# A decoder layer with a second cross attention: a new order of the same work on four engines

## The chip, the cores and the metric

The kernel runs on one core of one Trainium2 chip, in one launch. A core has a matrix engine (TensorE, PE in the profile, its weight loads PEld), three engines for elementwise work (VectorE or DVE, ScalarE or ACT, GpSimd or POOL) and a queue that issues the transfers (SyncE, SP). Each takes its instructions strictly in the order in which they are written, and waits on semaphores for the others. The metric is the device time of one execution in microseconds: median of three runs 888.63, lowest 887.2, highest 890.95.

## The reference

What is computed, for 64 sequences of 64 tokens with 256 features and 16 heads of 16:

```
def _L0(x, enc, self_mask, cross_mask, ...):
    q, k, v = split(layernorm(x, ln1) @ w_qkv + b_qkv)
    x = x + merge(attention(q, k, v, self_mask)) @ w_ao + b_ao
    q = layernorm(x, ln2) @ w_q + b_q
    k, v = split(enc @ w_kv + b_kv)
    x = x + merge(attention(q, k, v, cross_mask)) @ w_co + b_co
    return x + gelu(layernorm(x, ln3) @ w1 + b1) @ w2 + b2        # w1: 256 x 1024
def _L1(x, enc, mask, ...):
    a = norm(enc) * ln_gamma + ln_beta
    out = softmax(where(mask, (x @ Wq.T) (a @ Wk.T)^T * scale, -inf)) (a @ Wv.T)
    return x + tanh(gate) * (out @ Wo.T)
x = _L1(_L0(x, ctx, mask1, mask2, ...), ctx, mask3, ...)
```

Scores are `scores * mask - 10000 * (1 - mask)` in the first two attentions; everything is float32.

## The kernel before, in words

The 64 sequences are 16 units of 4 (256 tokens). A unit passes four working stages in four successive rounds: A is the self attention, B the first cross attention, M the MLP with the keys' and values' side of the second one, C the second cross attention. P, ahead of A, is the norm of the loaded tokens. In a full round (`steady`, 13 of them, the last without P) all stages work, each on another unit. Rounds 0 to 3 (`fill0` to `fill3`) fill the pipeline, `drain1` to `drain3` empty it. During `fill1` and `fill2` the weights are split into a high part (ScalarE, `high_weights`) and a low part (VectorE, `low_weights`).

Each matrix product of a projection is made of three: high times high, high times low, low times high. So an operand is turned on TensorE (`turn`), its high part is written by ScalarE (`high_part`), its low part by VectorE (`low_part`), and a projection (`feature_major` for queries, keys and the MLP's four inner parts H0 to H3; `token_major` for values and outputs) is twelve matmuls, of which the last four wait for the low part.

An attention x goes through these steps. TensorE: `scores(x, t)`, two halves of two pieces each. VectorE: `mask_scores(x, r)` for piece r = 0 to 3, `row_max`. GpSimd: `add_offset` (A and B), `shift` (subtract the row maximum). TensorE: `turn_probs(x, r)`, the transposed piece. ScalarE: `exps`, the exponential. TensorE: `values(x, t)`. VectorE: `normalise`. TensorE: `turn_out` (x.OT), then ScalarE's and VectorE's high and low part of it, then the output projection x.AO. VectorE's `tokens_out` adds the residual that GpSimd prepared (`residual`), `moments` takes mean and variance, GpSimd's `rstds` the inverse root, ScalarE's `normalised` applies both. The MLP: `gelus` on ScalarE, `high_h` on VectorE, `low_h` on GpSimd, then `mlp_out(t, part)` on TensorE.

What the order hangs on: every engine's list for each kind of round is written out by hand in `fill1` ... `drain3`. Two tables go with them. `PJ_ORDER` says in which order projections and turns claim the four projection banks of PSUM; a use waits until the use four places earlier has been read out (`claim`). `S_ORDER` says the same for the four score banks, which the scores and the turned pieces of A, B and C share. The keys `k2` and queries `q2` are one buffer each for all three attentions, so A's keys wait for B's scores. A and C share the buffer of probabilities. `keep_busy` is four transposes whose result nobody reads. `carry_shifts` makes bias columns out of the norms' shifts and the weights; `finish_biases` adds them up on VectorE.

## Time and profile before

| what | value |
|---|---|
| median of three runs | 888.63 us (887.2 to 890.95) |
| the profiled execution | 887.42 us, its span 885.6 us, mean granted TensorE clock 0.99 |
| TensorE matmuls, weight loads | busy 850.9 us (96%), 813.2 us (92%) |
| VectorE, ScalarE, GpSimd | busy 660.4 (75%), 573.8 (65%), 557.4 us (63%) |
| DMA | 26.76 MB, mean 30 GB/s |
| longest waits in total | GpSimd for the variance 200.3 us, ScalarE for the turned output 88.3, GpSimd for C's row maxima 82.7 |
| table loads on ScalarE | 63 of 1.28 us |

The span runs from the first to the last instruction; the execution's own time is 1.8 us more. Busy times of different engines overlap, so they are not parts of a sum. An engine's idle time costs nothing unless the engine that sets the end waits for it. The first filling round ends near 43.6 us, the second near 84, the third at 130.1; the full rounds run to 792.9, the first emptying round to 834.8, the second to 862.6.

### The profile page before, as it was taken

The numbers are of one execution on the slowest core, as the hardware profiler recorded it, in microseconds if no ns is written. First come the engines' busy times: TensorE is split into PE (matmuls) and PEld (weight loads), VectorE is DVE, ScalarE is ACT, GpSimd is POOL, SyncE is SP. The second block draws the span as 40 slices with busy tenths as digits, with TensorE's granted clock in tenths as the row PEclk, the third lists the DMA queues.
The fourth block names the chain that finished last, engine by engine and source line by source line (L and its number), as shares of the span: only waits on it lengthen the run. The fifth ranks groups of instructions, "written<-read, shape, count | busy, mean of one in ns | idle before, by whom it ended". The sixth has DMA issues, their size and how long they took to land.

```text
span 885.6 us, 24680 instructions
## 1 busy us (share of the span) xinstructions
PE 850.9 (96%) x9940; PEld 813.2 (92%) x9940; DVE 660.4 (75%) x1474; ACT 573.8 (65%) x1083; POOL 557.4 (63%) x565
## 2 busy tenths in 40 slices
PE   7878999999999999999999999999999999999996
PEld 7877889999999999999999999999999999998885
DVE  5868758778787777877777778778787787778454
ACT  5544858577584848758484866758485775848443
POOL 1456756749294765929486683938567492956351
PEclk9889999999999999999999999999999999999999
DMA  9010100100101010110101010010101001010000
GB/s 298 7 31 15 45 1 14 46 13 9 49 3 45 14 45 13 32 28 2 44 14 45 13 46 14 2 46 13 45 13 46 14 7 39 2 45 2 27 13 13
DMA packets 34143, 26.76 MB, mean 30 GB/s; under 512 B 12784, under 2 KB 33392, under 8 KB 34032
## 3 DMA queue, kind: packets, MB, share of 16 engines
q1 hardware_dynamic: 34032, 25.20, 9.8%
q8 instruction: 80, 1.31, 0.6%
q14 instruction: 31, 0.25, 0.1%
HBM read 20.99 MB, written 4.19 MB: 28 GB/s over the span
## 4 chain that ended last, share of the span: by engine, by line
POOL 44%; PE 34%; DVE 10%; issue 6%; ACT 4%; DMA 0%; POOLq 0%; SPq 0%; DVEq 0%; ACTq 0%
POOL prob_AC L1897 11%; POOL prob_B L1891 8%; POOL h_lo L1904 8%; POOL prob_AC L1891 8%; POOL prob_B L1897 5%; PE s_bank L566 5%; PE s_bank L541 4%; PE pj L439 3%; PE pj L492 3%; POOL rstd L1877 3%; PE pj L500 2%; PE pj L494 2%; PE pj L470 2%; PE pj L478 2%; PE pj L472 2%
## 5 line engine op out<-in xcount | busy, mean ns | idle before, releaser
L1877 POOL TENSOR_TENSOR rstd<-var_eps,half 128x2 f32<-128x2 f32 x64 | 45.5, 711 | 200.3 <-DVE var_eps L1402 200.3
L1897 POOL TENSOR_TENSOR prob_AC<-prob_AC,rmax_C 128x512 f32<-128x512 f32 x64 | 68.5, 1072 | 82.8 <-DVE rmax_C L1356 82.7
L1008 ACT ACTIVATE prob_AC<-s_bank 128x512 f32<-128x512 f32 x128 | 73.7, 616 | 70.7 <-PE s_bank L552 70.5
L1000 ACT ACTIVATE k<-pj,kbias,consts 128x256 f32<-128x256 f32 x192 | 92.7, 566 | 31.2 <-PE pj L478 26.6
L541 PE MATMUL s_bank<-k,q 64*128 64x128 f32 x1536 | 102.0, 282 | 6.3 <-ACT q L987 4.4
L541 PEld LDWEIGHTS s_bank<-k,q 64*128 64x128 f32 x1536 | 91.9, 190 | 13.6 <-ACT q L987 4.8
L1891 POOL TENSOR_TENSOR prob_AC<-prob_AC,maskA_off 128x512 f32<-128x512 f32 x64 | 81.5, 1286 | 15.0 <-DVE prob_AC L1351 15.0
L1891 POOL TENSOR_TENSOR prob_B<-prob_B,maskB_off 128x512 f32<-128x512 f32 x64 | 82.2, 1295 | 6.8 <-DVE prob_B L1351 6.5
L960 ACT ACTIVATE oT_AC_hi<-pj,bias 128x256 fp32r<-128x256 f32 x64 | 26.9, 472 | 88.3 <-PE pj L579 88.3
L1904 POOL TENSOR_TENSOR h_lo<-g,h_hi 128x512 fp32r<-128x512 f32 x64 | 82.4, 1296 | 1.2 <-DVE h_hi L1862 1.2
L552 PE MATMUL s_bank<-consts,prob_AC 128*128 128x128 f32 x512 | 72.9, 275 | 9.0 <-POOL prob_AC L1897 7.8
L552 PEld LDWEIGHTS s_bank<-consts,prob_AC 128*128 128x128 f32 x512 | 56.7, 140 | 16.5 <-issue 13.8
L1365 DVE RECIPROCAL rden<-s_bank 128x16 f32<-128x16 f32 x96 | 24.5, 256 | 61.6 <-PE s_bank L566 61.2
L1897 POOL TENSOR_TENSOR prob_B<-prob_B,rmax_B 128x512 f32<-128x512 f32 x64 | 69.0, 1088 | 0.8 <-DVE rmax_B L1356 0.8
L566 PEld LDWEIGHTS s_bank<-vz_AC,prob_AC 128*64 128x64 f32 x2048 | 62.6, 138 | 6.8 <-issue 4.0
L566 PE MATMUL s_bank<-vz_AC,prob_AC 128*64 128x34 f32 x2048 | 66.5, 225 | 1.4 <-issue 0.7
L513 PE MATMUL pj<-w_hi_M,h_hi 128*128 128x256 f32 x256 | 67.8, 298 | 0.0
L470 PE MATMUL pj<-zT_M_hi,w_hi_M 128*128 128x256 f32 x256 | 66.5, 293 | 0.0
L1897 POOL TENSOR_TENSOR prob_AC<-prob_AC,rmax_A 128x512 f32<-128x512 f32 x64 | 65.9, 1050 | 0.7 <-DVE rmax_A L1356 0.6
L472 PE MATMUL pj<-zT_M_hi,w_lo_M 128*128 128x256 f32 x256 | 63.6, 282 | 0.0
L514 PE MATMUL pj<-w_lo_M,h_hi 128*128 128x256 f32 x256 | 63.5, 282 | 0.0
L987 ACT ACTIVATE q<-pj,qbias,qscale 128x256 f32<-128x256 f32 x128 | 62.4, 590 | 0.8 <-PE pj L478 0.8
(209 smaller groups left out, 2690.5 us busy)
## 6 DMA issues: line engine op xcount, KB each, us to landing
x_in<-in_x SPq DMA_DIRECT2D x16, 256.0 KB, 2.8
ctx_b<-in_ctx_features SPq DMA_DIRECT2D x16, 256.0 KB, 3.0
ctx_c<-in_ctx SPq DMA_DIRECT2D x16, 256.0 KB, 3.0
out<-y SPq DMA_DIRECT2D x16, 256.0 KB, 2.2
maskB<-in_mask_Bx1xSxS_ff SPq DMA_DIRECT2D x32, 64.0 KB, 2.7
g<-in_w_M SPq DMA_DIRECT2D x2, 512.0 KB, 6.5
prob_AC<-in_w_A_qkv SPq DMA_DIRECT2D x3, 256.0 KB, 4.2
prob_B<-in_w_B_kv SPq DMA_DIRECT2D x2, 256.0 KB, 4.2
```

Source lines behind the costliest of these rows:

```text
L470: nc.tensor.matmul(bank[:, m * TOK:(m + 1) * TOK], w_hi[w][:, k, at], hi[:, k, :], start=(m == 0 and k == 0), stop=False)
L472: nc.tensor.matmul(bank[:, m * TOK:(m + 1) * TOK], w_lo[w][:, k, at], hi[:, k, :], start=False, stop=False)
L513: nc.tensor.matmul(bank[:, 0:H], h_hi[:, k, at], w_hi["M_2"][:, k, :], start=(k == 0), stop=False)
L541: mm = nc.tensor.matmul(bank[:, c, :, b2, :], q2[rows_, c, t * TILE + b2].rearrange("p e q -> p (e q)"), k2[rows_, c, t * TILE + b2], star ...
L552: last = nc.tensor.transpose(s_bank[r][:, n * P:(n + 1) * P], prob[a][:, r, n, :], ident[:, :])
L566: mm = nc.tensor.matmul(s_bank[t * HALVES][e * S:(e + 1) * S, m * TILE * VW:(m + 1) * TILE * VW], prob[a][:, t * HALVES + half, n, e * S:( ...
L1000: last = nc.scalar.activation(k2[:, m, :, s, :], k_all[:, m], ACT.Identity, bias=kbias[:, "ABC".index(a), s, m:m + 1], scale=parity[:, 2 + ...
L1008: nc.scalar.activation(prob[a][:, r, :, :].rearrange("p n k -> p (n k)"), s_bank[r][:, :], ACT.Exp).then_inc(turned_in[a], 1)
L1877: nc.gpsimd.tensor_tensor(rstd[:, n, :], var_eps[:, n, :], half[:, :], ALU.pow).then_inc(ln_rstd[l], 1)
L1891: nc.gpsimd.tensor_tensor(p3, p3, of_tile(maskA_off if a == "A" else maskB_off, a, r), ALU.add).then_inc(offset[a], 1)
L1897: nc.gpsimd.tensor_tensor(p3, p3, rmax[a][:, r, :].unsqueeze(2).broadcast_to([P, BL * TILE, S]), ALU.subtract).then_inc(shifted[a], 1)
L1904: nc.gpsimd.tensor_tensor(h_lo[:, 2 * m:2 * m + 2, :], g[:, m, :, :], h_hi[:, 2 * m:2 * m + 2, :].bitcast(F32), ALU.subtract).then_inc(h_l ...
```

## The change

The arithmetic, the buffers, the transfers and the semaphores stay as they are. In every kind of round the calls on TensorE, ScalarE, VectorE and GpSimd stand in another order, and the two tables follow. On TensorE, C's query projection stands directly behind its keys in full rounds; the first transposed piece of C stays ahead of A's keys, the other three now stand behind the fourth inner projection H3, and A's queries behind them; M.V stands between the third and the fourth piece of B. Fillers: four `keep_busy` open the kernel where six stood, and of those in the other rounds some go and some are moved. Some calls move from the head of one round's function to the tail of the one before. Nothing else is added.

```
-    "steady": ["C.xT", "C.K", "A.zT", "C.Q", "B.V", "M.zT", "B.zT", "B.K", "B.Q", "M.H0", "M.H1", "M.H2",
...
+    "steady": ["C.xT", "C.K", "C.Q", "A.zT", "B.V", "M.zT", "B.zT", "B.K", "B.Q", "M.H1", "M.H0", "M.H2",
...
             def fill0(i):
-                keep_busy("P.cA", i + 1)
...
+                keep_busy("A.zT", i + 1)
...
             def fill1(i):
-                carry_shifts("A", i, 0, 3)
                 pe.wait_ge(ln_done["A"], unit("A", i) + 1)
                 turn("A.zT", z["A"], i)
+                keep_busy("P.cA", i)
+                carry_shifts("A", i, 0, 3)
+                carry_shifts("A", 1, 1, 3)
...
                 turn_probs("A", 0, i)
+                carry_shifts("M", 1, 2, 4)
                 turn_probs("A", 1, i)
-                values("A", 0, i)
+                carry_shifts("M", 1, 3, 4)
...
-                carry_shifts("M", 1, 2, 4)
                 turn_out("A", i)
                 keep_busy("A.AO", i)
                 token_major("A.AO", i)
-                token_major("B.V", i + 1)
             def fill2(i):
-                carry_shifts("M", 1, 3, 4)
+                keep_busy("A.zT", i)
+                pe.wait_ge(ln_done["A"], unit("A", i) + 1)
+                turn("A.zT", z["A"], i)
+                token_major("B.V", i)
                 feature_major("B.K", i)
...
                 feature_major("B.Q", i)
-                feature_major("A.Q", i)
                 feature_major("A.K", i)
                 scores("B", 0, i)
                 scores("B", 1, i)
+                feature_major("A.Q", i)
                 scores("A", 0, i)
...
             def fill3(i):
-                token_major("B.V", i)
                 pe.wait_ge(ln_done["M"], unit("M", i) + 1)
                 turn("M.zT", z["M"], i)
+                token_major("B.V", i)
...
                 turn("B.zT", z["B"], i)
-                feature_major("M.H0", i)
...
                 feature_major("B.Q", i)
-                feature_major("M.H1", i)
+                feature_major("M.H0", i)
                 scores("B", 0, i)
...
             def steady(i):
...
                     feature_major("A.K", i)
-                    feature_major("A.Q", i)
+                if active("M", i):
+                    feature_major("M.H3", i)
                 if active("C", i):
                     turn_probs("C", 1, i)
                     turn_probs("C", 2, i)
                     turn_probs("C", 3, i)
-                if active("M", i):
-                    feature_major("M.H3", i)
-                if active("A", i):
+                if active("A", i):
+                    feature_major("A.Q", i)
                     token_major("A.V", i)
...
             def drain1(i):
...
                 token_major("M.V", i)
+                pe.wait_ge(tokens["M"], T * (unit("C", i + 1) + 1))
+                turn("C.xT", x3, i + 1)
+                pe.wait_ge(ln_done["M"], unit("M", i + 1) + 1)
+                turn("M.zT", z["M"], i + 1)
+                feature_major("C.K", i + 1)
             def drain2(i):
-                pe.wait_ge(ln_done["M"], unit("M", i) + 1)
-                turn("M.zT", z["M"], i)
-                pe.wait_ge(tokens["M"], T * (unit("C", i) + 1))
-                turn("C.xT", x3, i)
-                feature_major("C.K", i)
...
-                keep_busy("M.Y0", i)
-                keep_busy("M.Y0", i)
                 values("C", 0, i)
```

ScalarE, the head of the kernel. `z_A` is the normalised first unit, `w_hi_*` are high parts of weights, `zT_A_hi` is the high part of the turned `z_A`. Before:

```order
L934 ACT_TABLE_LOAD
L934 ACTIVATE w_hi_A_qkv<-prob_AC,consts 128x256 x6
L1016 ACTIVATE z_A<-x_in,mrstd,rstd 128x256 x2
L937 ACTIVATE w_hi_A_o<-prob_AC 128x512
L955 ACTIVATE zT_A_hi<-pj 128x512
```

And in the changed kernel:

```order
L1015 ACT_TABLE_LOAD
L1015 ACTIVATE z_A<-x_in,mrstd,rstd 128x256 x2
L933 ACTIVATE w_hi_A_qkv<-prob_AC,consts 128x256 x4
L954 ACTIVATE zT_A_hi<-pj 128x512
L933 ACTIVATE w_hi_A_qkv<-prob_AC,consts 128x256 x2
L936 ACTIVATE w_hi_A_o<-prob_AC 128x512
```

The norm moved ahead of six conversions, and two of the six behind the turned high part.

ScalarE, the middle of a full round. `g` is a gelu, `prob_AC` an exponential of C here, `k` and `q` are A's keys and queries, `cT_C_hi` and `oT_AC_hi` the high parts of M's turned context and of C's turned output. Before:

```order
L1008 ACTIVATE prob_AC<-s_bank 128x512
L1000 ACTIVATE k<-pj,kbias,consts 128x4x64 x4
L987 ACTIVATE q<-pj,qbias,qscale 128x4x64 x4
L1008 ACTIVATE prob_AC<-s_bank 128x512 x3
L1029 ACT_TABLE_LOAD
L1029 ACTIVATE g<-pj,bias 128x256 x2
L960 ACTIVATE oT_AC_hi<-pj,bias 128x256 x2
L1008 ACT_TABLE_LOAD
L1008 ACTIVATE prob_B<-s_bank 128x512
L955 ACTIVATE cT_C_hi<-pj 128x512
```

And in the changed kernel:

```order
L1007 ACTIVATE prob_AC<-s_bank 128x512 x2
L999 ACTIVATE k<-pj,kbias,consts 128x4x64 x4
L1007 ACTIVATE prob_AC<-s_bank 128x512 x2
L986 ACTIVATE q<-pj,qbias,qscale 128x4x64 x4
L1028 ACT_TABLE_LOAD
L1028 ACTIVATE g<-pj,bias 128x256 x2
L954 ACTIVATE cT_C_hi<-pj 128x512
L1015 ACTIVATE z_A<-x_in,mrstd,rstd 128x256 x2
L959 ACTIVATE oT_AC_hi<-pj,bias 128x256 x2
L1007 ACT_TABLE_LOAD
L1007 ACTIVATE prob_B<-s_bank 128x512 x4
```

A's keys moved behind C's second exponential and its queries behind all four; the context's high part and the norm `z_A` moved ahead of the high part of C's output.

GpSimd, the softmax run of a full round. `x<-x,brow` and `xb_A` are residuals, `rmax_C`, `rmax_B` and `rmax_A` mark the shifts of the three attentions, `mask*_off` the offsets, `h_lo` the low parts of the MLP's hidden layer. Before, to the end of the run:

```order
L1904 TENSOR_TENSOR h_lo<-g,h_hi 128x512
L1897 TENSOR_TENSOR prob_B<-prob_B,rmax_B 128x512 x2
L1904 TENSOR_TENSOR h_lo<-g,h_hi 128x512 x2
L1891 TENSOR_TENSOR prob_AC<-prob_AC,maskA_off 128x512
L1897 TENSOR_TENSOR prob_B<-prob_B,rmax_B 128x512
L1891 TENSOR_TENSOR prob_AC<-prob_AC,maskA_off 128x512 x2
L1897 TENSOR_TENSOR prob_AC<-prob_AC,rmax_A 128x512 x2
L1891 TENSOR_TENSOR prob_AC<-prob_AC,maskA_off 128x512
L1897 TENSOR_TENSOR prob_AC<-prob_AC,rmax_A 128x512 x2
```

And in the changed kernel:

```order
L1897 TENSOR_TENSOR prob_B<-prob_B,rmax_B 128x512
L1904 TENSOR_TENSOR h_lo<-g,h_hi 128x512
L1891 TENSOR_TENSOR prob_AC<-prob_AC,maskA_off 128x512 x2
L1897 TENSOR_TENSOR prob_B<-prob_B,rmax_B 128x512
L1891 TENSOR_TENSOR prob_AC<-prob_AC,maskA_off 128x512
L1897 TENSOR_TENSOR prob_AC<-prob_AC,rmax_A 128x512
L1891 TENSOR_TENSOR prob_AC<-prob_AC,maskA_off 128x512
L1904 TENSOR_TENSOR h_lo<-g,h_hi 128x512
L1897 TENSOR_TENSOR prob_AC<-prob_AC,rmax_A 128x512 x3
```

The low part of the fourth inner projection moved from ahead of A's offsets to between its first and its second shift.

## Rows read from the trace of the kernel before

**Rows 1.** The page, busy times: us (share of the span) xinstructions, by engine.

```profile
PE 850.9 (96%) x9940; PEld 813.2 (92%) x9940; DVE 660.4 (75%) x1474; ACT 573.8 (65%) x1083; POOL 557.4 (63%) x565
```

**Rows 2.** Stretches: length, busy us by engine, TensorE's clock, DMA share, GB/s.

```profile
0.00:43.60 43.60, 35.69 (x301) 33.60 (x302) 29.60 (x69) 23.57 (x47) 12.79 (x18) 0.88 0.49 155
43.60:84.20 40.60, 32.18 (x368) 30.00 (x366) 30.19 (x63) 18.01 (x37) 23.36 (x22) 0.92 0.08 25
84.20:130.10 45.90, 43.03 (x466) 39.99 (x466) 32.33 (x79) 28.60 (x53) 32.16 (x34) 1.00 0.08 22
130.10:792.90 662.80, 657.79 (x7907) 633.40 (x7906) 513.59 (x1151) 454.66 (x858) 450.13 (x454) 1.00 0.09 25
...
792.90:834.80 41.90, 40.34 (x450) 37.63 (x449) 29.59 (x66) 27.52 (x50) 23.15 (x24) 1.00 0.05 15
834.80:862.60 27.80, 25.85 (x278) 24.93 (x277) 15.13 (x32) 14.49 (x27) 11.75 (x11) 1.00 0.03 11
862.60:885.60 23.00, 16.02 (x186) 13.70 (x184) 9.95 (x18) 6.92 (x13) 4.09 (x4) 1.00 0.04 12
```

**Rows 3.** Timeline of GpSimd in the filling rounds: start, us, [idle before <- releaser].

```profile
31.97 2.04 POOL L1897 TENSOR_TENSOR prob_AC<-prob_AC,rmax_A 128x512 f32<-128x512 f32 x2
...
57.43 4.16 POOL L1891 TENSOR_TENSOR prob_B<-prob_B,maskB_off 128x512 f32<-128x512 f32 x3 [6.34 <-DVE prob_B L1351]
...
75.76 1.05 POOL L1897 TENSOR_TENSOR prob_AC<-prob_AC,rmax_A 128x512 f32<-128x512 f32 x1 [0.61 <-DVE rmax_A L1356]
...
96.94 1.27 POOL L1891 TENSOR_TENSOR prob_B<-prob_B,maskB_off 128x512 f32<-128x512 f32 x1 [0.18 <-DVE prob_B L1351]
...
118.23 2.05 POOL L1897 TENSOR_TENSOR prob_AC<-prob_AC,rmax_A 128x512 f32<-128x512 f32 x2
```

**Rows 4.** Timeline of TensorE in the full round from 537.97 us.

```profile
537.97 0.60 PE L439 MATMUL pj<-consts,x 128*128 128x128 f32 x4
...
565.19 2.06 PE L541 MATMUL s_bank<-k,q 64*128 64x128 f32 x32
...
580.12 0.63 PE L552 MATMUL s_bank<-consts,prob_AC 128*128 128x128 f32 x4 [0.30 <-POOL prob_AC L1897]
```

**Rows 5.** Timeline of ScalarE at the kernel's head.

```profile
7.09 2.50 ACT L934 ACTIVATE w_hi_A_qkv<-prob_AC,consts 128x256 fp32r<-128x256 f32 x6
9.50 1.08 ACT L1016 ACTIVATE z_A<-x_in,mrstd,rstd 128x256 f32<-128x256 f32 x2
```

**Rows 6.** Timeline of VectorE, cross biases in the first filling round.

```profile
28.47 1.33 DVE L1305 TENSOR_SCALAR kbias<-bias,consts 128x2 f32<-128x2 f32 x1
...
29.84 0.22 DVE L1305 TENSOR_SCALAR kbias<-bias,consts 128x2 f32<-128x2 f32 x1
```

**Rows 7.** Timeline of TensorE where the first filling round ends.

```profile
37.61 1.71 PE L428 MATMUL pj<-consts,g 128*128 128x1 f32 x8
...
43.57 0.28 PE L492 MATMUL pj<-w_hi_B_kv,cT_B_hi 128*128 128x256 f32 x1
...
44.99 0.95 PE L428 MATMUL pj<-consts,g 128*128 128x1 f32 x8
```

**Rows 8.** Timeline of ScalarE in the middle of the same full round.

```profile
560.17 1.96 ACT L987 ACTIVATE q<-pj,qbias,qscale 128x256 f32<-128x256 f32 x4
561.97 1.62 ACT L1008 ACTIVATE prob_AC<-s_bank 128x512 f32<-128x512 f32 x3
563.61 1.28 ACT L1029 ACT_TABLE_LOAD   x1
564.90 0.84 ACT L1029 ACTIVATE g<-pj,bias 128x256 f32<-128x256 f32 x2
```

**Rows 9.** Timeline of TensorE, its two waits in the emptying rounds.

```profile
834.31 0.66 PE L439 MATMUL pj<-consts,z_M 128*128 128x128 f32 x4 [0.86 <-ACT z_M L1016]
...
849.66 0.63 PE L552 MATMUL s_bank<-consts,prob_AC 128*128 128x128 f32 x4 [1.33 <-POOL prob_AC L1897]
```

**Rows 10.** Timeline of GpSimd ahead of C's last shift there.

```profile
846.88 1.46 POOL L1904 TENSOR_TENSOR h_lo<-g,h_hi 128x512 fp32r<-128x512 f32 x1
```

More of the change, by code:

```diff
@@ L761, in steady @@
                     scores("A", 1, i)
+                if active("M", i):
+                    pe.wait_ge(ln_done["C"], unit("M", i) + 1)
+                    turn("M.cT", ctx_c, i)
                 if active("C", i):
@@ new lines, in fill1, with fill2 @@
+                finish_biases("M", 1)
+                dve.wait_ge(xb_done["A"], unit("A", i) + 1)
+                if unit("A", i):
+                    dve.wait_ge(xb_done["B"], unit("A", i))
+                    dve.wait_ge(ln_done["B"], unit("A", i))
+                tokens_out("A", "A.AO", x1, xb["A"], i)
+                dve.wait_ge(tokens["A"], unit("A", i) + 1)
+                free("A.AO", i)
+            def fill2(i):
+                dve.wait_ge(tokens["A"], unit("B", i) + 1)
+                moments("B", x1, unit("B", i))
+                low_weights("M.Y0a")
+                low_part("A.zT", i)
+                low_part("B.zT", i)
+                dve.wait_ge(maskb_s, 32 * (unit("B", i) + 1))
+                if unit("B", i):
+                    dve.wait_ge(offset["B"], R * unit("B", i))
+                nc.vector.tensor_scalar(maskB_off[:, :, :], maskB[:, :, :], 1.0, OFF, ALU.subtract,
+                                        ALU.mult).then_inc(maskb_off_s, 1)
+                value_rows("B", "B.V", i)
+                low_weights("M.Y0b0")
+                low_weights("M.Y0b")
+                low_weights("C.K")
+                dve.wait_ge(maskb_s, 32 * (unit("B", i) + 1))
+                dve.wait_ge(setup_lo, PIECE["B.AO"] + 1)
+                mask_scores("B", 0, i)
+                mask_scores("B", 1, i)
+                mask_scores("B", 2, i)
+                row_max("B", 0, i)
+                mask_scores("B", 3, i)
+                row_max("B", 1, i)
+                row_max("B", 2, i)
+                mask_scores("A", 0, i)
+                mask_scores("A", 1, i)
+                row_max("B", 3, i)
+                dve.wait_ge(x_in_s, 16 * (unit("P", i) + 1))
+                moments("A", x_in, unit("P", i))
+                mask_scores("A", 2, i)
+                mask_scores("A", 3, i)
+                row_max("A", 0, i)
+                row_max("A", 1, i)
+                row_max("A", 2, i)
+                value_rows("A", "A.V", i)
+                low_weights("C.Q")
+                row_max("A", 3, i)
+                normalise("B", 0, i)
+                normalise("B", 1, i)
+                low_weights("C.AO")
+                low_part("B.OT", i, BV["B"])
+                normalise("A", 0, i)
+                normalise("A", 1, i)
+                dve.wait_ge(xb_done["B"], unit("B", i) + 1)
+                if unit("B", i):
+                    dve.wait_ge(xb_done["M"], unit("B", i))
+                    dve.wait_ge(ln_done["M"], unit("B", i))
+                tokens_out("B", "B.AO", x2, xb["B"], i)
+                dve.wait_ge(tokens["B"], unit("B", i) + 1)
+                free("B.AO", i)
+                moments("M", x2, unit("B", i))
+                low_part("A.OT", i, BV["A"])
@@ L1992, in steady @@
                     rstds("B", i, "B")
+                    pool.wait_ge(ln_done["B"], unit("B", i) + 1)
+                    residual("B", x1, 1, unit("B", i))
                 if active("A", i):
```

726 lines of the change are left out of this document (331 added, 395 removed).

## The prediction

> **What bounds the kernel now.** I read four things, in this order. First the page's busy times: TensorE is busy 850.9 of 885.6 us [rows 1], so no other engine's work is the limit, and only the 35 us in which TensorE is not busy can be won by order. Then the stretches, one for each part of the pipeline [rows 2]: the reader is to see where these 35 us lie. The thirteen full rounds hold 662.80 - 657.79 = 5.0 us of them. The three filling rounds hold 7.9 + 8.4 + 2.9 = 19.2 us, and the emptying ones 1.6 + 2.0 + 7.0 = 10.5 us. The granted clock is 0.88 and 0.92 in the first two filling stretches, so TensorE stands at its lower level (1.2 GHz) for 2 x 0.12 x 43.6 = 10.5 us and 2 x 0.08 x 40.6 = 6.5 us there, and at 2.4 GHz in all others.
>
> Third, GpSimd in the filling rounds [rows 3]. It works through the softmax of a round in one run without a hole: the first ends at 31.97 + 2.04 = 34.01, the second goes from 57.43 to 76.81 (19.4 us), the third from 96.94 to 120.28 (23.3 us). In between it waits for the next scores, 23.4 and 20.1 us. So filling is a chain: run, then values, output projection, layer norm, queries, scores, next run. Fourth, a full round: the one wait of TensorE there is 0.30 us in front of the last transposed piece of the self attention, for GpSimd's last subtraction [rows 4]. The rounds are 662.8 / 13 = 50.98 us long.
>
> The work is the same before and after but for the transposes that only keep TensorE busy. So each term below is a wait that goes or comes.
>
> **Filling, part by part.** First softmax run. The normalisation of the first tokens now stands ahead of the six weight conversions, which hold it from 7.09 to 9.50 [rows 5]. At most these 2.4 us go, and 1.6 if the first table load now waits for the norm. But the weight shifts now follow the turn on TensorE, and the key projection needs the biases made from them, so I let 0.5 us through. VectorE masks three pieces before it turns to a weight. Yet the last row maximum now stands behind the cross biases: such an operation took 1.33 us beside a GpSimd run and its twin 0.22 without [rows 6]; the four together may take 3 us, as now. Bounds for the end of this run: 0 to 3.3 us earlier (the second if the biases ran free); taken 1.1, near the case where they are held.
>
> From the first run to the second, 23.4 us. (a) The eight inner-weight columns between the values and the turned output (1.71 us at the low clock [rows 7]) move ahead of the third transposed piece, as does one of the fillers near them; the division in between takes about 1.2 us anyway, so 1.6 go. (b) Between cross queries and cross scores stand both self projections. A projection is twelve matmuls, 44.99 - 43.57 = 1.42 us [rows 7]; one of the two moves behind the scores, 1.4 to 1.5 us. (c) The turn of the next tokens and a filler move ahead of the cross turn, 0.9 us. (d) VectorE takes its low parts in the order in which TensorE asks for them, about 0.8 us. Sum 4.8; bounds 1.4 (only b) and 6.
>
> The second run has the same sixteen operations and keeps its 19.4 us; its bounds are -1 and +1, for the self masks must be there when its sixth operation ends.
>
> From the second to the third, 20.1 us. The cross values no longer stand ahead of the turn of the MLP's input, and the two inner projections that stood on both sides of the cross queries are now one, ahead of the scores. The value projection behind the turn hides the wait for the cross norm. I get one projection less, 1.5 us, bounds 0 and 3.
>
> Third run to the first full round, 9.8 us. The run loses one of its norms and two of four low-part subtractions to the time behind it, so its end comes 0.7 us earlier against its start; but the second output half of the MLP then waits for those two, 1.1 us. Together 0, bounds -1 and +1; fillers that fall away are in these bounds.
>
> The filling sum is 1.1 + 4.8 + 0 + 1.5 = 7.4 us, and with the lengths that TensorE allows (19.2 us idle now) it can't be more than about 12.
>
> **Full rounds.** On GpSimd the cross residual and a norm (2.3 us) move ahead of the run, three pieces of C stand together, and the low part of the fourth inner projection moves into the self pieces. The run starts about 0.4 us later in the round and ends about 0.8 earlier than now, when it lets TensorE go 580.12 - 537.97 = 42.15 us into its round [rows 4]. So the 0.30 us wait goes or shrinks. What is late next: the cross output's high part now stands behind all four self exponentials, so its low part and the self division slip, and the turned self output may wait 0.3 us. I take 0.2 us less a round, 2.5 in all, bounds +13 (below) and -5.0.
>
> The tight queue is ScalarE's. From the second transposed piece of C it now runs: three exponentials 1.62, four key copies as long as the four of the queries, 1.96 each, table load 1.28, gelu 0.84 [rows 8], then the context's high part 0.6 (as one exponential), a normalisation 1.08 [rows 5], and the high part of C's output 0.84 (as a gelu): with what they overlap some 10.3 us. TensorE's blocks added up in the new order (a projection 1.42 to 1.5 [rows 7], scores or values 2.0, a turn 0.4 [rows 4]) put that piece 21.3 us into the round and C's output projection at 32.2: estimates. Slack 0.6 us, and 0.4 at the self scores for the queries.
>
> A row and a rule differ here. The exponentials end at 561.97 + 1.62 = 563.59, the table load starts at 563.61, and the gelu starts at 564.90, at its end [rows 8]: a switch costs 1.3 us. The Trainium skill, on the page "ScalarE: Activation LUTs" (What ACT_TABLE_LOAD costs), counts 1.38 us of draining besides the 1.28. By that the queue above would be 1.4 us longer and the projection 0.8 us late in every round, some +10 us in all; the measurement decides, and I leave it out.
>
> **Emptying.** Now the turn of the MLP's input waits 0.86 us for its norm [rows 9]; behind it stand another turn and C's keys. C's turn now goes first, and softmax of B is a gelu's low part earlier, so keys come about 1.4 us earlier. In the next round GpSimd takes a norm and a low part (1.46 us) ahead of C's last subtraction [rows 10], and TensorE waits 1.33 us for it [rows 9]. All four subtractions now stand together, and two fillers go: 1.6 us. In the last round VectorE's eight operations set the pace; nothing. Together 3.0, bounds 0 and 4.5.
>
> **Sum.** The profiled execution took 887.4 us, of which 885.6 are span; 887.4 - 7.4 - 2.5 - 3.0 = 874.5. The three runs shown have their median at 888.63, 1.2 above it; about 0.5%, 4.4 us, is what can be told from no change.
>
> **Rivals.** (1) Filling keeps its length: waits move from one place in it to another. For it speaks that runs two and three keep their 19.4 and 23 us; against it that the gaps between are longer than their longest necessary chain. If only (b) and half of emptying come: 887.4 - 1.4 - 2.5 - 1.5 = 882.
>
> (2) The clock. Sixteen opening fillers stand where 24 stood, and other fillers go in the tail. TensorE now has 17 us at the low level; it fell each time in a stretch with waits [rows 2]. Twice as many such us cost at most half of 17, 8.5 us: 874.5 + 8.5 = 883. One more spell as long as that of the second stretch (6.5) costs 3. "TensorE: Matmul & The Clock Gate" of the Trainium skill (What's actually happening) says that activity is what releases the throttle; by that rule fewer fillers give this rival, and the price stays the one from the rows.
>
> (3) Slower. ScalarE's queue decides in the full rounds: exponential two now waits for a transposed piece behind the fourth inner projection, and keys and queries stand behind it. If the queue is 1.5 us late at C's output projection, TensorE waits a whole us each round: 887.4 - 7.4 - 3.0 + 13 = 890; from 0.85 us a round on the gain is gone. The rule of the Trainium skill on table switches, above, would end here too; the rows leave it no chance of its own. Against it: ScalarE is busy 454.66 of 662.80 us [rows 2], and I find 0.4 to 0.6 us of slack.
>
> (4) Full rounds lose all their idle time: 887.4 - 7.4 - 5.0 - 4.5 = 870.5; with more from filling, 867.
>
> **Chances.** Forecast, 870 to 878: 0.5. Rivals 1 and 2 with a time of 878 to 884: 0.21. Rival 4 and beyond, under 870: 0.11. The same within 4.4 us, from rivals 1 and 2 together or a weak 3: 0.12. Slower: 0.06. So 0.82 faster, and the range 866 to 885 leaves out about 0.06 on the low side and 0.12 on the high one. It is as wide as the bounds on ScalarE's queue and the filling gaps.
>
> **What would show it.** Right: the second and third GpSimd runs start about 5.9 and 7.4 us earlier (51.5 and 89.6), the first full round begins at 122 to 123, rounds are 50.7 to 50.9 us, C's last subtraction of the second emptying round has no low part in front. Wrong: rounds above 51.2 with TensorE waiting for queries or for C's high output; a granted clock under 0.85 in the first stretch; a third run that starts after 94.

## The result, and the profile after

The changed kernel takes 895.25 us (median of 11 runs, 891.55 to 898.38), the kernel before 888.63 (884.8 to 891.2, 11 runs): ratio 1.0081, 95% interval 1.0063 to 1.0098. It is slower by 0.8%, 6.6 us, where I had forecast 874.5 us.

The profiled execution took 898.38 us, the longest of the eleven. Its page, first the busy times as in [rows 1], then TensorE's granted clock in 40 slices:

```profile
PE 859.7 (96%) x9924; PEld 823.5 (92%) x9924; DVE 687.5 (77%) x1474; ACT 572.7 (64%) x1083; POOL 566.6 (63%) x565
...
PEclk9887999999999999999999999999999999999996
```

TensorE is busy 8.8 us longer with 16 matmuls fewer. The stretches of the same trace, columns as in [rows 2]; the limits are the ends of the filling rounds, of the full rounds and of the emptying ones:

```profile
0.00:49.54 49.54, 41.25 (x308) 38.54 (x309) 29.80 (x69) 24.22 (x49) 14.52 (x18) 0.90 0.43 136
49.54:91.31 41.77, 34.58 (x362) 31.56 (x361) 29.98 (x63) 16.29 (x33) 23.52 (x23) 0.88 0.09 24
91.31:137.46 46.15, 43.04 (x466) 39.86 (x465) 32.67 (x76) 27.09 (x54) 31.71 (x34) 1.00 0.08 22
137.46:801.98 664.52, 657.03 (x7907) 635.61 (x7905) 538.51 (x1151) 453.76 (x857) 457.26 (x454) 1.00 0.09 25
801.98:843.27 41.29, 39.70 (x446) 37.35 (x445) 29.81 (x64) 27.25 (x51) 23.87 (x24) 1.00 0.05 15
843.27:869.87 26.60, 25.60 (x275) 24.66 (x274) 16.52 (x32) 15.85 (x29) 11.65 (x11) 1.00 0.03 11
869.87:896.60 26.73, 18.51 (x174) 15.89 (x172) 10.25 (x19) 8.19 (x14) 4.08 (x4) 0.73 0.03 11
```

Against [rows 2], with all three limits at a turn of `x`: filling 137.46 against 130.09, +7.4; full rounds 664.52 against 662.8, +1.7; two emptying rounds 67.89 against 69.75, -1.9; the last one 26.73 against 22.97, +3.8. That sums to the 11.0 us between the two spans. The medians lie only 6.6 apart: filling and the last round vary from run to run with the clock, as the experiments show, and this trace is of a long run.

GpSimd's three runs, as in [rows 3]:

```profile
38.28 1.04 POOL L1897 TENSOR_TENSOR prob_AC<-prob_AC,rmax_A 128x512 f32<-128x512 f32 x1 [0.95 <-DVE rmax_A L1356]
...
61.98 2.53 POOL L1891 TENSOR_TENSOR prob_B<-prob_B,maskB_off 128x512 f32<-128x512 f32 x2 [6.11 <-DVE prob_B L1351]
...
76.86 4.49 POOL L1897 TENSOR_TENSOR prob_AC<-prob_AC,rmax_A 128x512 f32<-128x512 f32 x4
...
104.00 1.28 POOL L1891 TENSOR_TENSOR prob_B<-prob_B,maskB_off 128x512 f32<-128x512 f32 x1 [4.73 <-DVE maskB_off L1526]
```

The first ends at 39.32 (34.01 before), the second goes from 61.98 to 81.35 (19.4 us, as before), the third starts at 104.00 (96.94 before). So 5.3 us are lost before the first run ends, 0.8 won in the first gap, 2.5 lost in the second, and 0.3 behind the start of the third.

TensorE at the kernel's head, start and length of blocks of matmuls:

```profile
3.69 3.67 PE L447 MATMUL pj<-consts 128*128 128x128 f32 x16 [3.69 <-DMA consts<-in_constants]
8.98 1.11 PE L440 MATMUL pj<-consts,z_A 128*128 128x128 f32 x4 [1.62 <-ACT z_A L1015]
9.89 1.06 PE L447 MATMUL pj<-consts 128*128 128x128 f32 x4
10.74 3.41 PE L429 MATMUL pj<-consts,prob_AC 128*128 128x1 f32 x16
...
18.65 0.55 PE L471 MATMUL pj<-zT_A_hi,w_hi_A_qkv 128*128 128x256 f32 x1 [0.24 <-DVE kbias L1305]
```

The 16 fillers end at 7.4, the normalised tokens come at 8.9, and TensorE waits 1.62 us. Sixteen columns then take 3.41 us. In the kernel before, 24 fillers end at 9.2, eight columns follow, the wait for the tokens is 0.63 us, and the same sixteen columns take 1.84:

```profile
3.97 5.25 PE L446 MATMUL pj<-consts 128*128 128x128 f32 x24 [3.97 <-DMA consts<-in_constants]
...
12.01 1.84 PE L428 MATMUL pj<-consts,prob_AC 128*128 128x1 f32 x16
```

So TensorE runs at 1.2 GHz there in the changed kernel and at 2.4 GHz before. The trace has no clock record ahead of 21.9 us (9.0 before), and the stretches count what is missing as 1.00; the spacing of matmuls (0.21 and 0.11 us) tells the level.

Full rounds. TensorE's waits from 137.46 to 801.98 us (for whom, us in total, times, longest):

```profile
PE s_bank L542 <- DVE o_C L1367: 7.2, 13, 0.8
PE pj L501 <- DVE oT_AC_lo L1321: 0.2, 1, 0.2
```

And in the kernel before, from 130.09 to 792.88 us:

```profile
PE s_bank L552 <- POOL prob_AC L1897: 4.3, 14, 0.4
```

The wait of [rows 4] for GpSimd's last subtraction is gone from this list, and a longer one, 7.2 us in all, has come for A's scores. Who is late there, in the round from 597.25 us; VectorE, then TensorE:

```profile
623.45 0.69 DVE L1356 TENSOR_REDUCE rmax_B<-prob_B 128x8 f32<-128x512 f32 x1 [0.55 <-POOL prob_B L1891]
624.05 0.25 DVE L1365 RECIPROCAL rden<-s_bank 128x16 f32<-128x16 f32 x1
624.33 0.42 DVE L1367 TENSOR_TENSOR o_C<-s_bank,rden 128x256 f32<-128x256 f32 x1
```

```profile
622.35 2.06 PE L567 MATMUL s_bank<-vz_AC,prob_AC 128*64 128x34 f32 x64
624.90 1.35 PE L542 MATMUL s_bank<-k,q 64*128 64x128 f32 x19 [0.49 <-DVE o_C L1367]
```

A's scores need the bank out of which VectorE normalises C's output. That normalisation stands behind B's last row maximum, which itself waits for an offset by GpSimd.

### The profile page after: what moved, and what is told of

Its sections match the earlier page's. It is cut to its first block, busy times and chain, and to the rows that moved or that the text cites. A ratio compares the mean times of both kernels' runs of the same rounds, so it can differ in the third digit from the quotient of the medians.

```text
span 896.6 us, 24648 instructions
## 1 busy us (share of the span) xinstructions
PE 859.7 (96%) x9924; PEld 823.5 (92%) x9924; DVE 687.5 (77%) x1474; ACT 572.7 (64%) x1083; POOL 566.6 (63%) x565
## 4 chain that ended last, share of the span: by engine, by line
PE 66%; POOL 18%; DVE 11%; issue 3%; ACT 2%; POOLq 0%; DVEq 0%; ACTq 0%
POOL prob_B L1891 8%; PE s_bank L542 8%; PE s_bank L567 8%; PE s_bank L553 6%; PE pj L479 5%; PE pj L471 5%; PE pj L473 5%; PE pj L501 4%; PE pj L493 4%; PE pj L440 4%; PE pj L495 4%; PE pj L514 3%; POOL h_lo L1904 3%; PE pj L515 3%; PE pj L518 3%
## 5 line engine op out<-in xcount | busy, mean ns | idle before, releaser
L999 ACT ACTIVATE k<-pj,kbias,consts 128x256 f32<-128x256 f32 x192 | 92.5, 565 | 29.7 <-PE pj L479 27.3
L542 PE MATMUL s_bank<-k,q 64*128 64x128 f32 x1536 | 99.9, 280 | 11.5 <-DVE o_C L1367 7.2
L1891 POOL TENSOR_TENSOR prob_AC<-prob_AC,maskA_off 128x512 f32<-128x512 f32 x64 | 85.2, 1342 | 18.3 <-DVE prob_AC L1351 18.3
L553 PE MATMUL s_bank<-consts,prob_AC 128*128 128x128 f32 x512 | 70.5, 280 | 5.2 <-POOL prob_AC L1897 4.6
L959 ACT ACTIVATE oT_AC_hi<-pj,bias 128x256 fp32r<-128x256 f32 x64 | 26.7, 470 | 74.2 <-PE pj L580 74.2
L567 PEld LDWEIGHTS s_bank<-vz_AC,prob_AC 128*64 128x64 f32 x2048 | 65.7, 143 | 6.7 <-issue 4.1
L567 PE MATMUL s_bank<-vz_AC,prob_AC 128*64 128x34 f32 x2048 | 69.6, 229 | 1.0 <-issue 0.7
L1356 DVE TENSOR_REDUCE rmax_B<-prob_B 128x8 f32<-128x512 f32 x64 | 43.4, 679 | 35.2 <-POOL prob_B L1891 35.2
```

Of the source, the lines that this page charges most:

```text
L542: mm = nc.tensor.matmul(bank[:, c, :, b2, :], q2[rows_, c, t * TILE + b2].rearrange("p e q -> p (e q)"), k2[rows_, c, t * TILE + b2], star ...
L553: last = nc.tensor.transpose(s_bank[r][:, n * P:(n + 1) * P], prob[a][:, r, n, :], ident[:, :])
L567: mm = nc.tensor.matmul(s_bank[t * HALVES][e * S:(e + 1) * S, m * TILE * VW:(m + 1) * TILE * VW], prob[a][:, t * HALVES + half, n, e * S:( ...
L999: last = nc.scalar.activation(k2[:, m, :, s, :], k_all[:, m], ACT.Identity, bias=kbias[:, "ABC".index(a), s, m:m + 1], scale=parity[:, 2 + ...
L1891: nc.gpsimd.tensor_tensor(p3, p3, of_tile(maskA_off if a == "A" else maskB_off, a, r), ALU.add).then_inc(offset[a], 1)
```

## The experiments

Twelve kernels ran. In this table "low" is the time at 1.2 GHz from the first filler to the first full round; "full" are the thirteen full rounds; times are of the profiled execution but for the median and the ratio to the kernel before. The kernel before was run again beside each group of experiments, with medians of 887.4 to 888.9 us; the ratio is to these runs.

| kernel | median | ratio (95%) | low | first full round | full | last round |
|---|---|---|---|---|---|---|
| before | 888.6 | 1 | 22.1 | 130.1 | 662.8 | 23.0 |
| changed | 895.3 | 1.0081 (1.0063 to 1.0098) | 38.7 | 137.5 | 664.5 | 26.7 |
| e1 | 892.7 | 1.0046 (1.0021 to 1.0071) | 26.4 | 132.3 | 664.3 | 26.7 |
| e2 | 889.8 | 1.0026 (1.0005 to 1.0047) | 27.8 | 132.8 | 662.5 | 23.0 |
| e3 | 893.0 | 1.0067 (1.0037 to 1.0096) | 33.8 | 136.1 | 664.7 | 26.7 |
| e4 | 893.2 | 1.0056 (1.0031 to 1.0081) | 38.6 | 137.8 | 664.4 | 23.0 |
| e5 | 887.6 | 0.9997 (0.9976 to 1.0017) | 29.7 | 134.6 | 659.5 | 26.7 |
| e6 | 894.4, one run | | 39.8 | 137.9 | 663.9 | 23.0 |
| e7 | 887.9 | 0.9986 (0.9966 to 1.0007) | 4.5 | 126.8 | 664.7 | 23.0 |
| e8 | 883.4 | 0.9936 (0.9912 to 0.9959) | 20.2 | 133.7 | 660.8 | 23.0 |
| e9 | 890.1 | 1.0004 (0.9982 to 1.0027) | 15.7 | 131.0 | 664.3 | 23.0 |
| e10 | 876.9 | 0.9872 (0.9847 to 0.9897) | 12.0 | 130.3 | 656.4 | 23.0 |
| e11 | 880.0 | 0.9907 (0.9875 to 0.9939) | 27.8 | 132.7 | 656.6 | 23.0 |
| e12 | 889.8 | 1.0023 (1.0000 to 1.0046) | 23.8 | 132.6 | 664.5 | 23.0 |

**e1, 24 opening fillers in the changed kernel.**

```
             def fill0(i):
+                keep_busy("A.zT", i + 1)
+                keep_busy("A.zT", i + 1)
```

> The changed kernel (895.25 us) with six calls of opening fillers, 24 transposes, where it has four calls, 16. Theory of the clock: 24 fillers last until the first normalised tokens are there, so TensorE doesn't stand still for 2 us between its 16th filler and the first turn, reaches 2.4 GHz near 9 us of the span and not near 22 us, and GpSimd's first softmax run ends 4 to 5.5 us earlier (at 34 to 35 us, now 39.3): 890 us, 889 to 892. Rival, the new order at the head is itself the cost (the turn and the column products for the biases stand in a row ahead of the keys): the first run ends within 1 us of now, 894.5 to 896.

Measured 892.66 us. The trace shows what the clock theory said of the place:

```profile
3.83 5.38 PE L447 MATMUL pj<-consts 128*128 128x128 f32 x24 [3.83 <-DMA consts<-in_constants]
9.00 0.99 PE L440 MATMUL pj<-consts,z_A 128*128 128x128 f32 x4
...
10.27 1.84 PE L429 MATMUL pj<-consts,prob_AC 128*128 128x1 f32 x16
```

No wait, columns in 1.84 us, first run ended at 34.2, first full round 5.1 us earlier. The median falls by only half of that, 2.6 us, to just outside the expected 889 to 892, and its twelve runs spread from 883.8 to 895.4, so the size over many runs is less certain than the place. The other traces of the new order confirm the place: GpSimd's first run ends at 38.0 to 39.9 us in the five with 16 opening fillers (changed, e3 to e6), and at 34.0 to 36.6 in the four with 24 (e1, e7, e8, e10).

**e2, 16 opening fillers in the kernel before** (two of its six calls out).

> The kernel before (888.63 us) with four calls of opening fillers where it has six, 16 transposes for 24, nothing else. Theory of the clock: the same fall as in the changed kernel, TensorE stays at 1.2 GHz for some 10 us more at the head, 892 to 894 us. Rival, the fillers count only together with the new order at the head: 888 to 889.5 us. By my forecast on record, which put no price on the eight fillers that go, also no change.

Measured 889.83 us, 0.26% over before, interval 0.05 to 0.47%. The direction is that of the clock, the size about half of the 3.4 to 5.4 us that I expected, and the time is nearer to the rival's 888 to 889.5 than to my 892 to 894. In the trace TensorE waits 2.01 us for the tokens and is then at 1.2 GHz from 11.4 to 21.6 us, and the first full round begins 2.7 us later. Eight fillers cost there too. Whether they cost less than in the changed kernel is open: the first full round moves by 2.7 us here and by 5.1 in e1, in single traces, but the ratios differ by 0.26% here and by 0.35% there, with intervals wider than the difference.

**e3, VectorE: C's first normalisation ahead of B's last row maximum.**

```
                     row_max("B", 2, i)
-                    row_max("B", 3, i)
                 if active("C", i):
                     normalise("C", 0, i)
+                if active("B", i):
+                    row_max("B", 3, i)
+                if active("C", i):
                     normalise("C", 1, i)
```

> The changed kernel with two steps of VectorE exchanged in full rounds: C's first normalisation stands ahead of B's last row maximum, the second one behind it. Theory: A's scores wait 0.55 us a round for this normalisation, because it stands behind a row maximum that waits for GpSimd's offset; without it 13 rounds are 0.45 to 0.55 us shorter, 6 to 7 us: 888.5 us, 887.5 to 890. Rival, the wait goes over to the transposed pieces of A, whose last subtraction by GpSimd is not earlier: 893 to 895 us with a wait on the pieces in the trace.

My theory fell, the rival held: full rounds 664.7 us, no gain. A's scores no longer stand in the list of waits, but the fourth transposed piece comes at the same place of the round. In the round from 595.83 us:

```profile
622.87 2.29 PE L542 MATMUL s_bank<-k,q 64*128 64x128 f32 x32
...
635.65 1.71 PE L553 MATMUL s_bank<-consts,prob_AC 128*128 128x128 f32 x12
637.20 0.60 PE L580 MATMUL pj<-consts,o_B 128*128 128x128 f32 x4
637.74 0.63 PE L553 MATMUL s_bank<-consts,prob_AC 128*128 128x128 f32 x4
```

637.74 - 595.83 = 41.91, and 639.24 - 597.25 = 41.99 in the changed kernel. GpSimd sets both: its last subtraction ends 0.14 us ahead of that piece in each. The list of waits leaves out gaps under 0.15 us, so it doesn't show what e3 still loses: the scores take 2.29 us here and 2.06 in e10, the twelve pieces 1.71 here and 1.47 in e5. Busy time hides it as well:

```profile
136.10:800.83 664.73, 663.50 (x7906) 636.36 (x7905) 535.26 (x1151) 454.65 (x857) 457.13 (x454) 1.00 0.09 25
```

By this row of e3 TensorE is busy 663.50 of 664.73 us, and yet later kernels do the same full rounds in 8 us less.

GpSimd's run in the changed kernel, first and last row, and under it the same two rows of the kernel before (round from 588.91):

```profile
613.35 1.29 POOL L1891 TENSOR_TENSOR prob_B<-prob_B,maskB_off 128x512 f32<-128x512 f32 x1 [1.31 <-DVE prob_B L1351]
...
635.95 3.15 POOL L1897 TENSOR_TENSOR prob_AC<-prob_AC,rmax_A 128x512 f32<-128x512 f32 x3
```

```profile
605.61 2.54 POOL L1891 TENSOR_TENSOR prob_B<-prob_B,maskB_off 128x512 f32<-128x512 f32 x2
...
628.77 2.06 POOL L1897 TENSOR_TENSOR prob_AC<-prob_AC,rmax_A 128x512 f32<-128x512 f32 x2
```

From B's first offset to A's last subtraction it is 25.75 us now and 25.22 before, for the same operations. A full round is the way to this run (16.10 us now, 16.70 before), the run (25.75 and 25.22) and TensorE's work from the last piece on (9.1 and 8.8), with 0.14 us between: 51.1 us now, 50.9 before, in these two rounds. TensorE's waits ahead of the last piece are spare time in it.

**e4, three more calls of fillers in the last round.**

```
             def drain3(i):
+                keep_busy("C.OT", i)
...
                 turn_probs("C", 1, i)
+                keep_busy("C.OT", i)
                 turn_probs("C", 2, i)
...
+                keep_busy("C.AO", i)
                 token_major("C.AO", i)
```

> The changed kernel with three more calls of fillers in the last emptying round: one more ahead of C's first transposed piece, one between its second and third, one ahead of the last output projection, the last two as in the kernel before. Theory of the clock: TensorE keeps 2.4 GHz to the end, the last round (now 26.7 us from the turn of x) is 23 to 23.5 us as before: 891.5 to 892.5 us. Rival, the last round is longer because scores and masks now come in another order: 894 to 896 us and the last round over 25.5 us at the full clock.

Last round 23.0 us, at clock 1.00, as the theory said; the median falls by 2.0 us, to 893.22, just outside the 891.5 to 892.5 expected. One reservation came later: without added fillers the last round of this order was 26.7 us in four traces (changed, e1, e3, e5) and 23.0 in two (e6, e12); with them it was 23.0 in all five (e4, e7, e8, e10, e11). So the fillers don't win 3.7 us in each run, only in those where the clock would fall.

**e5, the exchange of e3 and the next tokens' norm out of GpSimd's run.**

```
                     shift("A", 3, i)
+                if active("P", i):
+                    rstds("A", i, "P")
                 if active("B", i):
                     rstds("M", i, "B")
```

(the same call goes from ahead of `shift("B", 2, i)`, and ScalarE's `normalised("A", x_in, i)` behind the high part of `B.OT`)

> The changed kernel with two edits in full rounds: the exchange on VectorE (C's first normalisation ahead of B's last row maximum), and the norm of the next tokens (GpSimd's inverse root and shift, 0.97 us) behind A's four subtractions and not in the middle of the softmax run, with ScalarE's normalisation of these tokens behind the high part of B's turned output. Theory now: two chains of equal length start from GpSimd's run, one by C's normalisation to A's scores, one by A's last subtraction to the last transposed piece; a full round is the run (25.75 us) with what TensorE does ahead of it and behind it, 51.04 us. With both shortened TensorE has no wait left: 50.4 to 50.6 us a round, 6 to 8 us in all, 887 us (885.5 to 889.5). Rival, the round is as long as TensorE's own instructions in the new order make it, and the 0.6 us are shown as a wait only where one is: 50.95 to 51.05 us a round, 893 to 895 us.

**e6, the norm alone, without the exchange.**

> The changed kernel with the norm of the next tokens behind GpSimd's run alone, without the exchange on VectorE. Theory of two equal chains: A's scores still wait 0.55 to 0.6 us for C's normalisation, and rounds stay 50.95 to 51.05 us. Rival, GpSimd's run alone sets the round: rounds of 50.1 to 50.6 us.

e5 measured 887.60 us, as expected, but its rounds are 50.67 us, above the 50.4 to 50.6. e6 ran once, 894.44 us.

The two with e3 make a square. The median full round is 51.06 us with neither edit, 51.06 with the exchange alone, 51.00 with the norm alone and 50.67 with both; the full rounds together are 664.5, 664.7, 663.9 and 659.5 us. GpSimd's run ends 41.79, 41.79, 41.55 and 40.99 us into the round (medians). So the norm, 0.97 us of GpSimd's time in the run, shortens the run by only 0.24 us as long as A's scores wait. e6 keeps the wait for C's normalisation:

```profile
PE s_bank L542 <- DVE o_C L1367: 7.5, 13, 0.8
```

Two chains of equal length from the same run, then, as the theory had it: each edit alone is worth under 0.7 us in 13 rounds, both 5.1. What the theory missed was 0.2 us a round: in e5, too, A's scores take 2.29 us, and e10 shows that they wait for C's second normalisation.

**e7, fillers only**, in the first two filling rounds and the last round.

> The changed kernel with fillers alone added: 24 opening transposes for 16, the three calls in the last round, and in the first two filling rounds calls of four transposes where TensorE waits over 0.9 us (two ahead of the third and three ahead of the fourth transposed piece of the first self attention, two ahead of B's first turn and two behind it, four ahead of the self scores, four and one ahead of B's third and fourth piece). Theory of the clock: the spells at 1.2 GHz between 33 and 78 us (20.4 us in the run with 24 opening fillers) shrink to under half, the first full round begins at 126 to 129 us, time 882 to 887 us. Rival, the fall of the clock is not to be kept away by fillers of this size, or filling is as long as its chain through the other engines: the first full round begins at 131 to 133, 888 to 890 us.

887.86 us. The profiled execution (884.2 us) has no spell at 1.2 GHz from 8.5 to 882 us, and its first full round begins at 126.8. It is the fastest of twelve, though, and the median lies between my 882 to 887 and the rival's 888 to 890. Fillers of this size keep the clock up in some runs only: the mean granted clock was 1.00 in three of the twelve, at 884.2 to 884.8 us, and 0.990 to 0.998 in the others, at 885.1 to 891.1.

**e8, all of these edits together.**

> The changed kernel with the fillers and both edits in full rounds together. Theory: the gains add up, first full round at 126 to 129 us, 13 rounds of 50.4 to 50.6 us, last round 23 us: 875 to 880 us, under the kernel before (888.6) by over 1%. Rival (filling doesn't get shorter by the fillers, rounds do not either): 888 to 890 us.

883.36 us, faster than before by 0.64%, but not the 875 to 880 expected. In its trace the clock fell twice all the same (13.8 to 20.6 and 30.9 to 41.1 us), and the first full round begins at 133.7. There lies a trap: a filler takes about twice as long at 1.2 GHz, so a dozen of them ahead of a transposed piece are then themselves what it waits for. The dozen ahead of A's fourth piece, in e7 and then in e8:

```profile
32.64 1.47 PE L447 MATMUL pj<-consts 128*128 128x128 f32 x12
34.17 0.63 PE L553 MATMUL s_bank<-consts,prob_AC 128*128 128x128 f32 x4
```

```profile
38.69 2.67 PE L447 MATMUL pj<-consts 128*128 128x128 f32 x12
41.19 0.60 PE L553 MATMUL s_bank<-consts,prob_AC 128*128 128x128 f32 x4
```

GpSimd's last subtraction for this piece ends at 34.03 in e7 and at 36.58 in e8: the piece comes 0.14 and 4.6 us later.

**e9, both kinds of edit in the kernel before.** The calls of fillers named in the expectation, and the norm behind GpSimd's run.

> The kernel before (888.63 us) with the same two kinds of edit: fillers where TensorE waits in the first two filling rounds (two calls ahead of the first keys, two ahead of the first values, four calls in place of two ahead of the third piece, one ahead of the fourth, one ahead of B's first turn, two ahead of the self queries, eight ahead of the self scores, three each ahead of B's second and third piece), and the norm of the next tokens behind GpSimd's run in full rounds, ScalarE's normalisation behind A's exponentials. It tells the order from the clock: if the new order of the filling rounds is as good as the old one, the first full round begins at 126 to 128 us here as in the changed kernel with fillers (126.8); if the old order is better, at 122 to 125.5. Full rounds: if only GpSimd's run held the old order, the 0.30 us wait goes and rounds are 50.5 to 50.6 us (sum 658 to 660 us); if they are as long as TensorE's own work, 50.85. Time 880 to 884 us with both.

890.12 us, no gain. The first full round begins at 131.0 with 15.7 us at the low level. Rounds went from 50.86 to 51.0, which neither of my two cases had. The wait moved to B's transposed pieces; from 131 to 795 us the longest is

```profile
PE s_bank L552 <- DVE prob_AC L1376: 2.2, 12, 0.2
```

What helps the new order doesn't help the old one.

**e10, e8 with both of C's normalisations ahead of B's last row maximum**, and two calls of fillers more ahead of the first keys.

```
                 if active("C", i):
                     normalise("C", 0, i)
+                    normalise("C", 1, i)
                 if active("B", i):
                     row_max("B", 3, i)
-                if active("C", i):
-                    normalise("C", 1, i)
```

> The changed kernel with all fillers and the norm behind the run (883.36 us in that run), two calls of fillers more ahead of the first keys, and both of C's normalisations ahead of B's last row maximum. In the run before this one A's second half of scores still waited 0.23 us for C's second normalisation. Theory: this wait goes, rounds 50.4 to 50.5 us where they were 50.67 to 50.77, 3 to 4 us less in 13 rounds: 879 to 881 us. Rival, GpSimd's run ends no earlier and B's last subtraction, a row maximum later, makes the pieces late: 50.65 us or more a round, 883 us.

876.92 us, 1.28% under the kernel before (interval 1.03 to 1.53%), the fastest of all; rounds are 50.43 us. Its stretch of full rounds:

```profile
130.28:786.66 656.38, 656.03 (x7906) 635.55 (x7905) 535.08 (x1151) 455.02 (x857) 457.48 (x454) 1.00 0.09 26
```

TensorE is busy 656.03 of 656.38 us. Whether order alone can win more there is open: e3 and e5 (659.09 of 659.46 us) look as full, and e10 is still 8.3 and 3.1 us shorter, since short waits count as busy.

**e12, the old filling rounds in the changed kernel, and e11, the same in e10.** The four engines' lists `fill0` to `fill3` and the two tables' entries are those of the kernel before.

> The changed kernel with the filling rounds of the kernel before alone put back, nothing else. It sums my account of the 6.6 us: filling costs 7.4 of them (5 by the clock), full rounds 1.7, the emptying rounds give 1.9, the low clock in the last round costs 3.7. Then the time is 895.25 - 7.4, 887 to 889.5 us with the scatter of filling, the same as the kernel before plus up to 3 us: 887.5 to 892, the first full round at 129 to 133 us, last round 26.7 us if the clock falls there again. Rival, most of the loss lies elsewhere: over 893 us.

> The run with all edits (876.92 us) with the filling rounds of the kernel before in all four engines' lists and both tables, without added fillers there (24 opening ones, as before). Full rounds, emptying and tail fillers stay. Theory: the new order of the filling rounds gains nothing at the same clock; the old filling ends near 130.1 us of the span, so the time is 874.5 to 878 us, equal to the run with the new filling and its fillers (whose first full round began at 126.8 to 133.7 us, by how long TensorE stood at 1.2 GHz). Rival, the new filling with fillers is worth 3 us and more: over 879 us.

e12: 889.83 us, as expected. So the new filling rounds cost 5.4 of the 6.6 us in the medians, and full and emptying rounds together 0.23% (0 to 0.46%). e11: 879.99 us. That is in the rival's range, over 879, and outside my 874.5 to 878, but its interval overlaps that of e10; whether the new filling with fillers is worth 3 us or nothing stays open.

## Why the prediction was wrong, point by point

**What bounds the kernel**: right. Filling is a chain over GpSimd's runs, and e3 and e5 show that a full round is one too. But I read a full round's end only at TensorE's one wait [rows 4], and counted the wait as all that could be late. And GpSimd's runs in filling are not without a hole, as I wrote: before the change it waits 0.96 us inside the first, for masked scores, and 0.61 inside the second, for a row maximum [rows 3].

**First softmax run, forecast 1.1 us earlier, measured 5.3 later.** Of this, the order is the smaller part. With 24 fillers (e1) the run starts 1.1 us earlier than before but takes 11.3 us where it took 10.0, and ends 0.2 later, so the forecast 1.1 is not there even then. VectorE's last row maximum for A begins only at 32.42 us in e1, behind two low parts of weights (2.36 us) and the cross biases (2.4), and GpSimd waits 0.95 us for it. The other 5.1 us are the clock. I had put the eight fillers that go into rival 2 and priced them by the 17 us at the low level that the stretches show, when the first 9 us, which they miss, are just those in which fillers bring the clock up. I had also moved the first norm ahead of the conversions without asking what TensorE would do until it came: it has nothing, since the column products that filled this place now stand behind.

**The gaps between the runs, forecast -4.8 and -1.5.** Measured -0.8 and +2.5. With no spell at the low level (e7: 34.0 to 53.8, and 72.6 to 93.3 us) they are 19.7 and 20.7 us against 23.4 and 20.1. The kernel before has 6.8 us at 1.2 GHz in the first gap, so part of the 3.7 us there is the clock's and not the order's; no run separates the two. In the second, where it has none, there is indeed one projection less, but TensorE now waits in four places, 1.4 us in all (in the changed kernel and in e7), for queries and for high and low parts that it asks for sooner, where it waited in two for 0.8 us; the rest of the missing 2.1 us I can't assign.

**Filling as a whole, forecast -7.4, measured +7.4.** The table helps to tell order and clock apart. Without many added fillers, the new order begins its full rounds at 132.3, 134.6, 136.1, 137.5, 137.8 and 137.9 us with 26.4, 29.7, 33.8, 38.7, 38.6 and 39.8 us at the low level: 0.42 us for each of them. The old order has 130.1, 132.6, 132.7 and 132.8 with 22.1, 23.8, 27.8 and 27.8. At 27 to 28 us both stand near 132.8. So at the same clock the new order shows no gain, and 16.7 more us at 1.2 GHz at 0.42 are 7.0 of the 7.4, an estimate. These are single traces with a scatter of over 1 us about the line, and a spell at the low level also follows from waits, so the line alone doesn't prove its price; what is shown on its own is the head (e1, e2), and the filling's 5.4 us in the medians (e12). Added fillers are not free: the same line carried on to 4.5, 12.0 and 20.2 us gives 123.1, 126.3 and 129.7, and e7, e10 and e8 stand some 4 us above it.

**Full rounds, forecast -2.5, measured +1.7.** This is the other step that failed. I feared ScalarE's queue and added it up; no wait of TensorE over 0.15 us is for it. I didn't add up VectorE's, which the change had moved as well, and there B's last row maximum now stands ahead of C's normalisation, where it stood behind. The 0.30 us wait did go. But I had GpSimd's run start 0.4 us later in the round and end 0.8 earlier; it starts 0.6 earlier (16.10 against 16.70), is 0.5 longer and ends where it did (41.79 against 41.93, medians), and TensorE's part behind it is 0.3 longer. Rival 4, full rounds without idle time in the list of waits, was real after all: e10 has it, by two edits that the change lacked.

**Emptying, forecast -3.0, measured -1.9 and +3.8.** The places named came as forecast: the turns ahead, and no low part ahead of C's last subtraction; the waits of 0.86 and 1.33 us are gone. But shorter ones took their place, so TensorE's idle time in these two rounds falls only from 3.5 to 2.6 us, and its busy time by 0.9 with the two calls of fillers that went. The last round, costed at nothing, lost 3.8 us in this trace to the clock: 0.73 there, where [rows 2] has 1.00.

**Which rival held.** The second, the clock, with a bound too low (I allowed 8.5 us against my forecast) and together with the first. The step that failed first is this price: the fillers at the head were taken at nothing in the sum, and at most at half of 17 us in the rival. A fall by clock and order together below the kernel before was not among my cases, since the slower one hung on ScalarE alone. Of the wrong signs that I named, one showed: the third run starts after 94 us, at 104.0. Rounds are 51.1 us, not above 51.2, and TensorE waits in them for C's normalisation, not for queries or C's high output. The clock of the first stretch reads 0.90, not under 0.85, but only because what is missing counts as 1.00: with the 18.2 us from the first filler to the first record at the low level it is 0.71.

The Trainium skill, "TensorE: Matmul & The Clock Gate" (What's actually happening), says that activity releases the throttle, and that the same kernel shows different numbers of slow matmuls from run to run. By that rule fewer fillers pointed to rival 2. The trace agrees: 1.84 or 3.41 us for the same sixteen columns, by eight fillers, and first full rounds between 126.8 and 133.7 us in e7 and e8, whose filling is the same.

## What to carry to other kernels

Before a list is rewritten, find the cycle that a steady round closes (here GpSimd's softmax run), and check each engine's queue ahead of what TensorE asks for next, not only the one that looks full. Where two chains from the same source are equally long, each fix alone shows nothing; test them together before dropping either. Don't take an empty list of waits, or a busy share near 100%, as proof that TensorE is the limit: compare how long the same block takes in two kernels. Fillers are part of the design at the head and the tail: the work that hides a wait while the clock is still low is worth what the clock is worth, and one trace with its own luck must be set against many runs.

## What the runs showed of the hardware that I had not expected

The same 52 casts of VectorE take 508 ns each in full rounds before and 947 in the changed kernel, 23.8 us more in all, of the 24.9 us by which VectorE is busier:

```profile
L1862 DVE CAST h_hi<-g 128x512 fp32r<-128x512 f32 x52 | 25.4, 508 | 0.2 <-issue 0.2
```

```profile
L1862 DVE CAST h_hi<-g 128x512 fp32r<-128x512 f32 x52 | 49.2, 947 | 0.0
```

One takes 0.43 us in the kernel before (at 604.77 us, beside a small operation of GpSimd) and 1.51 in the changed one beside GpSimd's low parts (at 618.28 us), and there two low parts take 2.70 us, where two took 2.53 before. The Trainium skill, "GPSIMD Engine Reference" (Key points), names such contention between GpSimd and VectorE for some of VectorE's modes; that it is this rule which acts on the casts is argued, not tested. It may be one reason why GpSimd's run got longer; no experiment priced it apart.

Single executions of one kernel differ by over 10 us (e1: 883.8 us at a mean granted clock of 0.996, 895.4 at 0.974), more than the whole effect of the change.
